# Node sums of both parities in one PSUM bank, and 14 unread bf16 matmuls a step in the bank set free (graph attention)

## The reference

```python
h = (x @ W).reshape(N, H, C)
alpha_s = jnp.einsum('nhc,hc->nh', h, a_src)
alpha_d = jnp.einsum('nhc,hc->nh', h, a_dst)
e = jax.nn.leaky_relu(alpha_s[src] + alpha_d[dst], NEG_SLOPE)
m = jax.ops.segment_max(e, dst, num_segments=N)
ex = jnp.exp(e - m[dst])
den = jax.ops.segment_sum(ex, dst, num_segments=N)
alpha = ex / (den[dst] + 1e-16)
out = jax.ops.segment_sum(h[src] * alpha[:, :, None], dst, num_segments=N).reshape(N, H * C) + b
x = jax.nn.relu(out)
```

## Time and profile before

| What | us |
|---|---|
| median of 3 runs | 8691.24 |
| lowest and highest run | 8664.57, 8694.72 |
| profiled execution, from first to last instruction | 10523.1 |
| PE busy (matmuls) | 5795.2 |
| DVE busy | 4507.0 |
| ACT busy | 3562.3 |
| POOL busy | 6521.8 |

### The profile page before, as it was taken

One profiled execution on the slowest core, in us unless ns is written; L12 is line 12 of the kernel. 1 busy time (PEld: TensorE's weight loads), 2 busy tenths in 40 slices (PEclk: granted clock), 3 DMA queues, 4 the chain that ended last, 5 costly groups with the idle time before them and its releaser, 6 DMA issues. The chain is left out here.

```text
span 10523.1 us, 129592 instructions
## 1 busy us (share of the span) xinstructions
PE 5795.2 (55%) x27752; PEld 5101.0 (48%) x27752; DVE 4507.0 (43%) x11640; ACT 3562.3 (34%) x7369; POOL 6521.8 (62%) x6545
## 2 busy tenths in 40 slices
PE   4666666676755555545545555555554545545453
PEld 2155555665644444444444544444444444444443
DVE  6644545455533333333343333333334333333335
ACT  3611111111233333333333333333333333333333
POOL 3455666666366666666656666666665666666665
PEclk6555555555556666666666666666666666666666
DMA  4211111111111111111121111111112111111111
GB/s 130 49 32 36 39 38 39 38 39 39 29 35 34 35 34 34 34 35 34 34 34 35 34 34 34 34 34 35 34 32 36 34 35 34 34 35 34 34 34 30
DMA packets 290251, 394.16 MB, mean 37 GB/s; under 512 B 176393, under 2 KB 183961, under 8 KB 287985
## 3 DMA queue, kind: packets, MB, share of 16 engines
q0 software_dynamic: 206976, 330.75, 16.5%
q1 hardware_dynamic: 61176, 46.25, 1.8%
q10 hardware_dynamic: 22024, 16.47, 0.7%
HBM read 367.38 MB, written 25.63 MB: 37 GB/s over the span
## 5 line engine op out<-in xcount | busy, mean ns | idle before, releaser
L637 POOL DMA_INDIRECT store<-table_a,idx x4851 | 4835.4, 997 | 2626.8 <-issue 1595.4
L1262 PE MATMUL ps<-ident,work 128*128 128x128 f32 x4872 | 1179.2, 417 | 2359.3 <-issue 2226.4
L1279 PE MATMUL ps<-store,work 128*128 x9744 | 1788.8, 355 | 1176.6 <-ACT work L1211 841.1
L1279 PEld LDWEIGHTS ps<-store,work 128*128 128x128 f32 x9744 | 1655.2, 263 | 1379.5 <-issue 1377.7
L778 POOL DMA_INDIRECT store<-table_m,idx x1617 | 1597.5, 988 | 1130.6 <-issue 554.9
L1262 PEld LDWEIGHTS ps<-ident,work 128*128 128x128 f32 x4872 | 928.6, 218 | 2456.7 <-issue 2336.8
L1218 ACT ACTIVATE work<-work,small 128x896 f32<-128x896 f32 x696 | 724.5, 1041 | 3314.6 <-issue 2135.0
L1155 DVE SCALAR_TENSOR_TENSOR work<-dstf,store,select 128x224 f32 x696 | 314.2, 451 | 3116.2 <-issue 1668.3
L1144 DVE CUSTOM_DVE_ANT_0 work<-work,ps 128x896 f32<-128x896 f32 x696 | 756.8, 1087 | 1258.7 <-issue 937.7
L1270 PE MATMUL ps<-ident,work 128*128 128x128 f32 x4872 | 1100.6, 398 | 105.7 <-issue 73.9
L870 PE MATMUL ps<-work 128*128 128x96 f32 x3248 | 817.6, 443 | 615.0 <-DVE work L1058 439.8
(11 more groups left out here) (250 smaller groups left out, 4865.7 us busy)
## 6 DMA issues: line engine op xcount, KB each, us to landing
store<-table_a,idx POOLq DMA_INDIRECT x4851
store<-table_m,idx POOLq DMA_INDIRECT x1617
work<-edge_parts ACTq DMA_DIRECT2D x232, 45.5 KB
edge_parts<-store SPq DMA_DIRECT2D x6, 1617.0 KB, 11.7
work<-edge_parts SPq DMA_DIRECT2D x50, 192.0 KB
table_a<-work SPq DMA_DIRECT2D x12, 606.0 KB, 6.5
work<-table_b ACTq DMA_DIRECT2D x232, 12.0 KB
idx<-in_src_dram SPq DMA_DIRECT2D x116, 28.0 KB
```

The lines of the kernel that those rows point to most:

```text
L637: pool.indirect_dma_start(rows[:, k % RING, j, 0:width], None, table, bass.IndirectOffsetOnAxis(ap=idx[:, k // CHUNK, at:at + 1], axis=0)) ...
L1262: last = pe.transpose(ps[:, 4 + j // 4, (j % 4) * P:(j % 4 + 1) * P], prob[:, par, j, :], ident[:])
L1279: last = pe.matmul(ps[:, 6 + par, 0:D + 1], probT[:, par, j, :], rows_of(at("slot", 3))[:, j, 0:D + 1], start=(j == 0), stop=(j == TPG - 1))
```

## The change

The sums of both parities go to bank 6, at columns 0 to 96 and 128 to 224. A new helper `keep_clock(pe, n)` issues n matmuls into bank 7, each with a 128-column bf16 view of `ident` as weights and 512 bf16 columns of `ident` as the moving operand; nothing reads what they write and they raise and await no semaphore. TensorE issues 3 between `turn_mask` and `weighted_sums` and 11 behind `weighted_sums`, in every step, also in the steps at a stage's start and end in which the others are left out.

```diff
@@ -581,6 +581,12 @@
+        def keep_clock(pe, n):
+
+            weights, moving = ident[:].bitcast(BF16)[:, 0:P], ident[:].bitcast(BF16).unsqueeze(1).broadcast_to([P, 2, 2 * P])
+            for _ in range(n):
+                pe.matmul(ps[:, 7, :].rearrange("p (b n) -> p b n", b=2), weights, moving, start=True, stop=True)
+
@@ -1222,7 +1228,7 @@
                 def parts(k, par, at):
                     act.wait_ge(s["o_ready"], k + 1)
                     for v in range(2):
-                        last = nc.scalar.activation(part_sums[:, par, v, :], ps[:, 6 + par, 0:D + 1], ACT.Copy,
+                        last = nc.scalar.activation(part_sums[:, par, v, :], ps[:, 6, P * par:P * par + D + 1], ACT.Copy,
                                                     scale=selects[:, bass.ds(at("table", 3) + WA + v, 1)])
@@ -1276,7 +1282,7 @@
                     for j in range(TPG):
-                        last = pe.matmul(ps[:, 6 + par, 0:D + 1], probT[:, par, j, :],
+                        last = pe.matmul(ps[:, 6, P * par:P * par + D + 1], probT[:, par, j, :],
                                          rows_of(at("slot", 3))[:, j, 0:D + 1],
                                          start=(j == 0), stop=(j == TPG - 1))
@@ -1285,8 +1291,10 @@
                         turn_probs(q - 3, (par - 3) % 2, at)
                     if live(1):
                         turn_mask(q - 1, (par - 1) % 2, at)
+                    keep_clock(pe, 3)
                     if live(3):
                         weighted_sums(q - 3, (par - 3) % 2, at)
+                    keep_clock(pe, 11)
                 return step
```

## The result

The changed kernel takes 8896.2 us (median of 4 runs, 8887.26 to 8913.23) against 8691.01 us for the kernel before (4 runs, 8664.57 to 8694.72): ratio 1.0249 (95% interval 1.0231 to 1.0266), 205 us slower. The time lies above the forecast of 8690 us and above the upper end of its range, 8850.

What follows compares the result with a forecast made beforehand. The prediction took POOL's row of gathers (floor 8604 us), not TensorE, to bound the kernel. It summed 8691 (timed median) + 0 (bank) + 0 (matmuls, covered) - 1 = 8690 us, with a range from 8590 to 8850 us.

Steps and rivals of the forecast that it cites:

- The timed kernel is POOL's row of gathers almost without a gap: POOL, all four stages: 6468 gathers at 1.25 us plus 519 us give 8604 us; timed runs have 87 us more.
- the recording of TensorE's many short instructions: First profile: recording them holds back TensorE's completions, a disturbance; the profile is 1832 us longer than the timed runs.
- 8604 us and the small remainder: Whole kernel unprofiled: the waits vanish, leaving POOL's gathers and other time, with 87 us on top.
- Rival 1: POOL's attention waits: held completions also real in timed runs, gathers cheaper; 7735 us, or 8210 for half; chance 0.12.
- rival 2: Attention: the 87 us are small waits for turn_mask, removed by nearly doubled slack at high clock; 8604 us; chance 0.08.
- the shared bank: `weighted_sums` and `parts` using bank 6 instead of banks 6 and 7: no wait added, cost 0.
- the three matmuls: Between turn_mask and the sums: cost nothing, covered by the wait for L1211; otherwise they delay the sums by 0.6 us.
- Which clock: TensorE in attention, averaging 0.63 to 0.64 before: high clock most of the time; signs say granted clock above 0.9.
- The eleven cost nothing, covered by the wait for the next landing: Behind the sums, before the second turn_probs: cost nothing; without that cover 2.3 us a step.
- L1279 some 1.8 us: Sign for the sums on TensorE in attention: 14 sums take 1.80 us at the high clock, 3.30 before.
- rival 3: Second turn_mask ends at 13.8 + 5.2 x us (x: low-clock share), late beyond 0.36; 8850 to 9120 us; chance 0.20.
- a late TensorE has no hole left: Argument against rival 3, in attention: once TensorE is late, no idle hole remains; no size given.

Runs made afterwards that it cites:

- the run with POOL's own work: Kernel with the shared bank alone, plus a small POOL memset and a wait for its end before each attention group's gathers: 9562.97 us, ratio 1.0998.
- POOL told earlier, ends removed: Changed kernel with the 14 matmuls only in steps having both mask and sums, and gather g waiting for mask g-3 instead of g-2: 8687.99 us, ratio 0.9994.
- the run with POOL told earlier: Changed kernel with the gather of group g waiting for the turned mask of g-3 instead of g-2: 8705.24 us, ratio 1.0016.
- the run with 14 ahead: Changed kernel with all 14 matmuls behind `turn_mask` and none behind the sums: 8708.54 us, ratio 1.0016.
- the run with 8 and 6: Changed kernel with eight matmuls behind `turn_mask` and six behind the sums, instead of 3 and 11: 8739.89 us, ratio 1.0062.

## Why the prediction was wrong

**The frame was right.** "The timed kernel is POOL's row of gathers almost without a gap": a microsecond more on POOL is a microsecond more in time (the run with POOL's own work). The 1832 us of the first profile belonged to that recording alone: the second profile of the same kernel doesn't have them, and timed runs never had. What was wrong there is the cause given. The prediction laid it to the recording of TensorE's many short instructions, and the same number of instructions was recorded again with nothing held back, then 149416 instead of 129592 as well. What held the completions in that one execution stays open. The Trainium skill ("NOTIFIC — the notification-queue block", 7.1) has the block hold its producers back; no run here shows when that sets in, and the sum that the prediction drew from it, 8604 us and the small remainder, is what second profile and timed runs show. Rival 1, which took the waits as real in timed runs, is excluded; rival 2 too: where POOL waits for no mask (POOL told earlier, ends removed), 0.9994 is no gain.

**Right as well:** the shared bank costs 0 (1.0009, interval from 0.9999), the three matmuls cost 0 (1.0004), the clock in attention rises to 0.90, and the added TensorE time is 2683 us of a forecast of 2070 to 4150.

**The step that failed** is under "Which clock": "I take the high clock for most of the time, and keep the other for a rival", and with it "The eleven cost nothing, covered by the wait for the next landing". The average clock did come out at 0.90. But the prediction had put a hole of 3.1 us before the sums and the 2.3 us of the eleven right behind it, and it took the mean clock for the clock at this place. The trace has the hole at 3.14 us, as worked out, and the clock falls in just such holes: 230 of the 262 blocks of sums behind a hole of 3.0 us or more ran at the low level, and the eleven behind them took a median of 3.45 us instead of 2.54. "L1279 some 1.8 us", one of the prediction's signs, failed in these steps. So the eleven didn't cost nothing: they and the slow sums brought the second `turn_mask` too late for POOL, and with POOL waiting for an earlier mask instead the time was 8705.24 us, not 8896.2. For the pair shown, rival 3's formula gives x = (16.6 - 13.8) / 5.2 = 0.54, well beyond its 0.36. The argument against rival 3, "a late TensorE has no hole left", holds only once TensorE is late: by then the low clock has done its harm, and 337 of 696 steps have the hole ahead of their sums all the same.

So **rival 3** happened, at its place and by its mechanism, with a chance of 0.20. Its price was put together differently: not 348 pairs late by 0.5 us (160 us), but 100 group starts, each late by 1.16 us on average (116 of the 165 us of pauses).

**Two terms were missing.** A late mask costs more than the wait at the group's first gather. In 56 groups the second gather comes after a pause that is 0.86 us longer than usual on average (49 us together). In 27 of them the first gather was late, in the other 29 it was on time; in all 56 `turn_mask` had ended less than 1.2 us before POOL's last gather of the group ahead, or after it. The gathers are longer too, by 25 us. So 165 + 25 - 116 = 74 us of the stages' 192 lie outside the first waits. And the matmuls at the ends of the stages lie beside no gather: 9 to 17 us. With 192 in the stages and these, the 205 us are accounted for within what the runs vary.

**Nothing was to be won either**, and there the prediction's sum held. The Trainium skill ("TensorE: Matmul & The Clock Gate", Terms) puts the penalty of the throttle at the throttled time multiplied by the share of the clock that is withheld. As an estimate by that page, from 0.66 to 0.91 in attention (throttled share 0.68 to 0.18, times a half, of 6088 us) the clock would give back some 1520 us. Rows say nearly as much of TensorE alone: its transposes and sums are busy 4038 us in the kernel before (L1262, L1270, L1279: 1156.2 + 1103.1 + 1778.7) and 2768 in the run with POOL told earlier (661.7 + 653.2 + 1453.1), 1270 us less. That run, at 0.91, gave 1.0016. The measurement decides: such a sum prices TensorE's time, and TensorE isn't what this kernel waits for. None of the versions run beats the kernel before.

## What to carry to other kernels

Filler work isn't placed by how much idle time an engine has, but by what ends that time: ahead of a wait for another engine it was nearly free (14 matmuls there, 1.0016), behind that wait and before something that the bottleneck needs it costs (11 there, 1.025), because it leaves open the hole in which the clock falls. Don't read a mean clock as the clock at the critical spot; look at the stretch right behind each hole. And when a profile's span and the timed runs are far apart, profile the same kernel again before reading any wait in it.

## What was not expected of the hardware

A single recording can be 1832 us off and look consistent. In the first one completions of TensorE reached the others late, by 7.2 us in the place of the earlier trace rows, and 588 waits through all stages were ended by "remote"; in the thirteen later recordings of this and the other kernels not one was. The cause wasn't found.

POOL's indirect gathers are 0.945 us long and 0.30 apart, and a disturbed group loses that rhythm once more. In the changed kernel it was the pause ahead of the second gather (56 times, 1.17 us on average instead of 0.30). That isn't simply the price of starting again, since 29 of the 56 groups had started on time. With POOL told one step earlier there was none, though the masks of g-2 were turned as late. In the run with POOL's own work it was the third gather, 1.57 us instead of 0.95: 622 of 693 took over 1.2 us. Whether the two are the same thing wasn't tried.

A hole of 3.14 us in otherwise dense work was enough for the clock to go from 0.96 to 0.50, and the low level outlasted it, through 3.30 us of sums and well into the 4.25 us behind them; with six matmuls instead of eleven it reached the next transposes (L1268 in 1.29 instead of 0.98 us). The holes of 0.92 us in the run with 14 ahead left it up. Between these, length alone doesn't tell: of the holes of 2.0 to 2.5 us, none of 35 in the changed kernel was followed by slow sums, and 89 of 136 in the run with 8 and 6 were.
